# A decoder layer on one core: x1 and x2 of 13 groups turned in 32x32 blocks on VectorE and moved by 16 transfers each, with another order of a round's products

## The reference

```python
qkv = x @ w_qkv.T + b_qkv                      # 8 heads, no softmax
x = layernorm(x + ((q @ k.T) @ v) @ w_o.T + b_o)            # x1
q, k, v = x @ W_q.T + b_q, ctx @ W_k.T + b_k, ctx @ W_v.T + b_v   # 16 heads of 32
attn = softmax(where(mask == 0, -1e9, q @ k.T / sqrt(32)))
x = layernorm(x + (attn @ v) @ W_o.T + b_o)                 # x2
x_prev = x shifted by one row within a batch
xr, xk = mu * x + (1 - mu) * x_prev
out = sigmoid(xr @ W_r.T) * (square(relu(xk @ W_k.T)) @ W_v.T)
x = layernorm(x + out)                                      # y3
```

## Time and profile before

| | |
|---|---|
| median of 3 runs | 916.45 us (916.25 to 916.95) |
| profiled execution | 914.96 us, its span 912.9 us |
| granted TensorE clock | 0.998 of full |
| busy: TensorE, VectorE, ScalarE, GpSimd | 98%, 76%, 61%, 57% |

### The profile page before, as it was taken

One profiled execution on the slowest core, in us unless ns is written; L12 is line 12 of the kernel. 1 busy time (PEld: TensorE's weight loads), 2 busy tenths in 40 slices (PEclk: granted clock), 3 DMA queues, 4 the chain that ended last, 5 costly groups with the idle time before them and its releaser, 6 DMA issues.

```text
span 912.9 us, 23290 instructions
## 1 busy us (share of the span) xinstructions
PE 896.7 (98%) x8774; PEld 749.0 (82%) x8774; DVE 695.6 (76%) x1994; ACT 556.5 (61%) x1667; POOL 521.8 (57%) x505
## 2 busy tenths in 40 slices
PE   8999999999999999999999999999999999999997
PEld 7867766787788888888878888888888888888886
DVE  6688566578877878787877878787877777787775
ACT  7555236858675756575856666666665757575631
POOL 1045015759666666666675757566676767665420
PEclk9999999999999999999999999999999999999999
DMA  8792020113000001012101010101010100100001
GB/s 296 245 271 58 24 94 2 43 36 136 9 25 31 25 25 31 24 32 82 32 24 32 24 32 25 32 25 32 25 32 24 31 26 12 44 2 24 2 24 46
DMA packets 32332, 46.54 MB, mean 51 GB/s; under 512 B 3806, under 2 KB 16606, under 8 KB 32094
## 3 DMA queue, kind: packets, MB, share of 16 engines
q1 hardware_dynamic: 28622, 37.99, 12.8%
q10 hardware_dynamic: 3600, 7.08, 2.3%
HBM read 34.10 MB, written 9.70 MB: 48 GB/s over the span
## 4 chain that ended last, share of the span: by engine, by line
PE 75%; DVE 4%; POOL 4%; issue 4%; ACT 1%; POOLq 0%; ACTq 0%
PE dense L92 19%; PE dense L94 17%; PE dense L93 17%; PE turned L1664 5%; PE turned L1686 5%; PE scores L1650 4%; PE dense L1540 2%; PE turned L1668 1%; PE turned L1540 1%; POOL row_inv L1442 1%; POOL weight L1450 1%; PE scores L1546 1%; DVE mix_k_raw L1204 1%; PE dense L1557 0%; POOL prob_rest L1449 0%
## 5 line engine op out<-in xcount | busy, mean ns | idle before, releaser
L1442 POOL TENSOR_TENSOR row_inv<-row_sum,minus_one 128x4 f32<-128x4 f32 x128 | 152.6, 1192 | 190.1 <-ACT prob L818 190.0
L818 ACT ACTIVATE prob<-prob,row_min 128x154 f32<-128x154 f32 x512 | 209.6, 416 | 39.8 <-DVE row_min L1160 39.8
L1450 POOL TENSOR_TENSOR weight<-prob,row_inv 128x512 f32<-128x512 f32 x128 | 148.0, 1156 | 0.0
L1160 DVE CUSTOM_DVE_ANT_0 prob<-scores,mask_add 128x154 f32<-128x154 f32 x512 | 127.8, 312 | 4.0 <-PE scores L1650 3.7
L826 ACT ACTIVATE prob_t<-turned 128x512 f32<-128x512 f32 x128 | 76.0, 594 | 84.6 <-PE turned L1664 83.8
L818 ACT ACTIVATION_READ_ACCUMULATOR prob<-prob,row_min 128x1 f32 x512 | 98.3, 192 | 0.0
L1664 PE MATMUL turned<-ident,weight 128*128 128x128 f32 x512 | 76.9, 272 | 3.4 <-DVE o_t_lo L1167 3.0
L1664 PEld LDWEIGHTS turned<-ident,weight 128*128 128x128 f32 x512 | 61.2, 139 | 17.9 <-issue 6.3
L92 PE MATMUL dense<-mix_k_hi,ffn_wk_hi 128*128 128x256 f32 x256 | 75.3, 294 | 0.0
L92 PE MATMUL dense<-xt_hi,cross_wq_hi 128*128 128x256 f32 x256 | 75.2, 294 | 0.0
L94 PE MATMUL dense<-mix_k_hi,ffn_wk_lo 128*128 128x256 f32 x256 | 72.3, 283 | 0.0
(11 more groups left out here) (276 smaller groups left out, 2684.7 us busy)
## 6 DMA issues: line engine op xcount, KB each, us to landing
x_rows<-x_rows SPq DMA_DIRECT2D x32, 256.0 KB, 4.6
xt_raw<-x_cols SPq DMA_DIRECT2D x16, 512.0 KB, 3.8
out<-gate_then_y SPq DMA_DIRECT2D x15, 512.0 KB, 2.8
mask_in<-mask SPq DMA_DIRECT2D x16, 154.0 KB, 2.3
cross_wv<-cross_wv SPq DMA_DIRECT2D x2, 512.0 KB, 6.6
cross_wk<-cross_wk SPq DMA_DIRECT2D x1, 1024.0 KB, 9.3
self_wv<-self_wv ACTq DMA_DIRECT2D x1, 1024.0 KB, 7.3
self_wk<-self_wk ACTq DMA_DIRECT2D x1, 1024.0 KB, 9.6
```

What stands on the lines that cost most here:

```text
L818: m = act.activation(keys, keys, ACT.Exp, bias=row_min[:, buf, t, h:h + 1], scale=-1.0, accum_out=row_sum[:, buf, t, h:h + 1])
L1160: m = dve.tensor_tensor_reduce(exp_slot(n, u)[:, i * CTX:(i + 1) * CTX], s_bank[:, h, t * CTX:(t + 1) * CTX], mask_add[n % 2][:, t, :], -S ...
L1442: pool.tensor_tensor(row_inv[:, buf, t, :], row_sum[:, buf, t, :], minus_one[:], ALU.pow).then_inc(*p_inv.up)
L1450: pool.tensor_tensor(first, early, inv_early, ALU.mult).then_inc(*p_norm.up)
```

## The change

For 13 groups each (x1 of groups 3 to 15, x2 of groups 1 to 13) the transposes on TensorE go. VectorE turns each tile in 32x32 blocks (`turn`, one instruction of 128x512 for a tile), x1 into a buffer over `xt_hi`, x2 into one over the second half of o_t, and SP then moves the blocks to the partitions where they belong: 16 transfers for x1 (into `x_in`) and 16 for x2 (into x2t), each of 32 partitions x 1 KB. x1 is then split from SBUF with one `x1_high` (ScalarE, 128x1024) and one `x1_low` (VectorE, 128x1024), which replace two instructions each; `turned_x2` goes. The turned x stays in blocks of 32 columns: `q_product` reads its moving operand in eight runs of 32 columns, `take_q` puts the columns back in order, and `difference` becomes two instructions. It is now x_prev - x, with 1 - mu made once in the column constants. The raw difference lies in the buffer of mix k, so `blend(f, "r")` comes first.

Products come in another order, bank assignments and their waits change with them, and ScalarE's, VectorE's and GpSimd's orders follow. Two waits are new in `v_product`'s second half and in `q_product`: the first now waits for `r_gate(e, 1)`, the second for `x1_low(a)` and for the first `v_finish(e, 0)`. `exponentials`, `take_turned` and the rest are as before. On GpSimd `x_low` comes first, `scale(2, f)` moves ahead of the second `weigh`, and `scale(3, e)` to the end of the same round.

```diff
-    tile["x2t"] = mem.place("x2_t", [P, KT, 1 + GT])
+    tile["x2t"] = mem.place("x2_t", [P, 1 + GT // SQUARE, KT, SQUARE])
+    tile["x2_squares"] = mem.over("o_t_hi", "x2_squares", [P, 3, D], 4 * D)
+    tile["x1_squares"] = mem.over("xt_hi", "x1_squares", [P, TPG, D])
...
+        steady = {"y": (d1, d0), "o": (d1, d0), "k": (d0, d1), "r": (d0, d1), "q": (d0, d0), "v": (d0, d1)}
+        in_loop = lambda kind, n: kind in steady and first_of[kind] <= n <= past[kind]
+        bank = lambda kind, n, i: (steady[kind] if in_loop(kind, n) else last.get((kind, n), two[kind]))[i]
...
+            def move_x1(n):
+                sp.wait_ge(*tr1_mm.at(n))
+                for j in range(ROWS4):
+                    for i in range(ROWS4):
+                        sp.dma_start(x_in[j * SQUARE:(j + 1) * SQUARE, i, :],
+                                     x1_squares[i * SQUARE:(i + 1) * SQUARE, :, j * P:(j + 1) * P]).then_inc(*x1_back.up)
+
+            def move_x2(n):
+                sp.wait_ge(*tr2_mm.at(n))
+                sp.wait_ge(*carried.at(n))
+                for j in range(ROWS4):
+                    for i in range(ROWS4):
+                        sp.dma_start(x2_places[j * SQUARE:(j + 1) * SQUARE, 1 + i:2 + i + ROWS4:ROWS4, :],
+                                     x2_squares[i * SQUARE:(i + 1) * SQUARE, 0:3:2, j * P:(j + 1) * P]).then_inc(*x2_back.up)
...
                 if live(e - 1) and e - 1 < LAST:
                     store(e - 1)
+                if live(f) and moved_x2(f):
+                    move_x2(f)
...
+            def x1_high(n):
+                act.wait_ge(*x1_back.at(n - 3))
+                act.activation(xt_hi[:], x_in[:], ACT.Copy).then_inc(*x1t_hi_ok.up)
...
+                if g >= 2 and moved_x2(n - 1):
+                    act.wait_ge(*x2_back.at(n - 2))
...
-                x_high(a)
                 k_relu_half(e, 0)
                 take_turned(n, 0, 0)
-                k_high(e, 0)
                 exponentials(n, 1, 0)
+                x_high(a)
                 take_turned(n, 0, 1)
...
-                r_gate(e, 0)
+                exponentials(n, 2, 1)
+                k_relu_half(e, 1)
+                o_high(n, 1)
                 if n == 2:
                     weight_high("ffn_wv")
-                turned_x2(f, 0)
-                r_gate(e, 1)
-                x1t_high(a, 0)
-                o_high(n, 1)
-                x1t_high(a, 1)
-                turned_x2(f, 1)
+                k_high(e, 1)
                 exponentials(n, 3, 0)
-                k_relu_half(e, 1)
+                r_gate(e, 0)
                 take_turned(n, 2, 0)
+                x1_high(a)
                 exponentials(n, 3, 1)
-                k_high(e, 1)
-                mix_high(f, "k")
-                take_q(a, 0)
-                if a == GPB - 1:
-                    next_m_high(0)
                 take_turned(n, 2, 1)
                 take_rest(n, 2)
-                if a == GPB - 1:
-                    next_m_high(1)
+                r_gate(e, 1)
                 mix_high(f, "r")
                 if a == GPB - 1:
-                    next_m_high(2)
-                take_q(a, 1)
+                    for k in range(KT):
+                        next_m_high(k)
+                take_q(a, 0)
                 o_high(n, 2)
-                if a == GPB - 1:
-                    next_m_high(3)
...
+
+            def turn(to, rows, t):
+                return dve.transpose(to.rearrange("p (j k s) -> p k j s", j=ROWS4, k=KT),
+                                     rows[:, t, :].rearrange("p (k j s) -> p k j s", j=ROWS4, k=KT))
+
+            def turn_x1(n):
+                dve.wait_ge(*y_mm.at(n))
+                for t in range(TPG):
+                    dve.wait_ge(*ln_ok[1].at(n, t + 1))
+                    turn(x1_squares[:, t, :], x1[n % 2], t).then_inc(*tr1_mm.up)
+
+            def turn_x2(n):
...
+            for n in range(2, LAST):
+                a, f, e = n + 1, n - 1, n - 2
+                o_low(f, 3)
+                masked_min(n, 1, 0)
+                masked_min(n, 1, 1)
+                k_square(e, 0)
+                k_low(e, 0)
...
+                o_finish(f, 0)
+                o_finish(f, 1)
+                o_low(n, 0)
+                masked_min(n, 2, 0)
+                normalise(2, f, x2[f % 2])
+                turn_x2(f)
...
+                y_finish(a, 0)
+                masked_min(n, 2, 1)
+                y_finish(a, 1)
+                normalise(1, a, x1[a % 2])
+                turn_x1(a)
+                k_square(e, 1)
+                o_low(n, 1)
+                masked_min(n, 3, 0)
+                masked_min(n, 3, 1)
...
+                k_low(e, 1)
+                make_mask(a)
+                difference(f)
+                x1_low(a)
+                blend(f, "r")
+                v_finish(e, 0)
+                blend(f, "k")
+                carry(f + 1)
+                o_low(n, 2)
+                masked_min(a, 0, 0)
+                masked_min(a, 0, 1)
+                k_mix_low(f)
...
+                v_finish(e, 1)
+                normalise(3, e, y3)
...
+            def spread_product(to, weight, h, parts):
+                for i in parts:
+                    cols = slice((2 * h + i) * P, (2 * h + i + 1) * P)
+                    for k in range(KT):
+                        m = three_pass(pe, to[:, i * GT:(i + 1) * GT].rearrange("p (b s) -> p b s", s=SQUARE),
+                                       (weight[0][:, k, cols], weight[1][:, k, cols]),
+                                       (moving(xt_hi)[:, k], moving(xt_lo)[:, k]), first=(k == 0), last=(k == KT - 1))
...
-                        pe.wait_ge(*k_sq.at(n - 3, 2))
-                m = column_product(bank("q", n, h), w["cross_wq"], (xt_hi, xt_lo), h, parts)
+                    pe.wait_ge(*(x1_low_at(n) if moved_x1(n) else x1t_lo_ok.at(n)))
+                    if h == 0 and n >= 3:
...
-                    pe.wait_ge(*q_out.at(n + 3, t + 1))
+                    pe.wait_ge(*r_out.at(n, t + 1))
...
-                y_product(a, 0)
                 values(n, 0)
                 scores(n, 2)
+                y_product(a, 0)
+                transposes(n, 1, 0)
                 y_product(a, 1)
-                transposes(n, 1, 0)
-                r_product(e, 0)
                 transposes(n, 1, 1)
-                r_product(e, 1, early)
-                x2_turn(f, 0)
-                r_product(e, 1, late_half)
-                x1_turn(a, 0)
+                k_product(e, 1)
                 values(n, 1)
                 scores(n, 3)
-                x1_turn(a, 1)
-                x2_turn(f, 1)
-                k_product(e, 1)
+                r_product(e, 0)
                 transposes(n, 2, 0)
+                r_product(e, 1)
+                transposes(n, 2, 1)
+                v_product(e, 0)
+                v_product(e, 1, early)
                 q_product(a, 0)
-                transposes(n, 2, 1)
-                q_product(a, 1)
                 values(n, 2)
                 scores(a, 0)
-                v_product(e, 0)
+                v_product(e, 1, late_half)
                 transposes(n, 3, 0)
-                v_product(e, 1, early)
+                q_product(a, 1, (0,))
                 transposes(n, 3, 1)
-                v_product(e, 1, late_half)
+                q_product(a, 1, (1,))
                 values(n, 3)
                 scores(a, 1)
```

More of the change, by code:

```diff
@@ L30 @@
 PIECES = P // SIDE_ROWS
+SQUARE = 32
+ROWS4 = P // SQUARE
 EPS = 1e-5
@@ L1000, in act_program @@
                 take_rest(n, 3)
-                exponentials(a, 0, 0)
+                take_q(a, 1)
                 exponentials(a, 0, 1)
@@ L1144, in x1t_low, with x1_low @@
             def x1t_low(n, t):
-                cols = slice(t * P, (t + 1) * P)
                 dve.wait_ge(*x1t_hi_ok.at(n, t + 1))
-                dve.tensor_tensor(xt_lo[:, :, cols], by_k(bank("x1", n, t)), f32(xt_hi[:, :, cols]),
+                dve.tensor_tensor(spread(xt_lo)[:, t], squares(bank("x1", n, t)), f32(spread(xt_hi)[:, t]),
                                   ALU.subtract).then_inc(*x1t_lo_ok.up)
+            def turn(to, rows, t):
[7 more added lines that the diff above has]
+            def turn_x2(n):
+                dve.wait_ge(*o_mm.at(n))
+                for t in range(TPG):
+                    dve.wait_ge(*ln_ok[2].at(n, t + 1))
+                    turn(x2_squares[:, 2 * t, :], x2[n % 2], t).then_inc(*tr2_mm.up)
+            def x1_low(n):
+                dve.wait_ge(*x1_high_at(n))
+                dve.tensor_tensor(xt_lo[:], x_in[:], f32(xt_hi[:]), ALU.subtract).then_inc(*x1t_lo_ok.up)
             def masked_min(n, g, t):
@@ L1177, in carry @@
             def carry(n):
-                first, last = x2t[:, :, 0:1], x2t[:, :, GT:GT + 1]
+                first, last = x2t[:, 0, :, SQUARE - 1:SQUARE], x2t[:, GT // SQUARE, :, SQUARE - 1:SQUARE]
                 if n:
@@ L1265, in dve_program @@
             take_t(0)
```

(33 more changed lines are left out.)

154 lines of the change are left out of this document (76 added, 78 removed).

## The result

The changed kernel takes 1067.44 us, the median of 4 runs (1065.26 to 1069.2), against 916.35 (4 runs): a ratio of 1.1646, 95% interval 1.1619 to 1.1673. It is slower, as forecast, but by 151 us and not by 61, and it lies above the range that was given. Its profiled execution took 1069.2 us, with a span of 1067.3.

The account below looks back on a forecast made before the run. TensorE's queue bounds the 47.0 us round; without turns 45.8, plus 5.9 of waiting for x1's moved blocks, makes 51.7. 914.96 + 13 x 4.7 = 976, with 1.5 for the median 977.5 us; range 925 to 1050.

Parts of the forecast that it names:

- The round without the wait for x1: TensorE's loop round if everything else arrives in time: 45.8 us, 1.2 a round less than before.
- short waits: Two waits left on TensorE by the order: 0.3 us for scores(a, 0), 0.2 at the last weight transposes.
- The runs of 32 columns: q_product's moving operand read in runs of 32 columns on TensorE, taken at no cost.
- A turn: VectorE's turn of one 128x512 tile: 0.69 us, 2.8 a round for four.
- x2's squares: VectorE has x2's turned blocks ready to move 4.7 us after the first y_product starts.
- From x1_high to TensorE's start: ScalarE's steps from x1_high through the gate r_gate(e, 1): 4.0 us.
- The one long wait: TensorE waits about 6 us a round before v_product's second half, released by ScalarE's gate.
- One issue and its gap: Price of each of the 32 transfers a round on SP's queue: 0.50 us, within bounds of 0.42 and 0.9.
- The landing behind the last issue: Time from the end of SP's issues until x1_high can start: 2.0 us.
- The Trainium skill's 50 ns of dispatch: Under this rule the moves take 2.8 us and the rival of transfers in time, 900 us, holds: 12%.
- the clock at 1.00: TensorE's granted clock in the rounds stays at 1.00; if it falls with the idle time, the loss is larger.
- x2 was said to be in time: x2's moved blocks are back at 14.7 us in the round, ahead of VectorE's difference at about 15.9.

Follow-up runs that it names:

- four_each: Changed kernel with each move made by 4 transfers of 128 KB in place of 16 of 32 KB, values landing in wrong places: 913.21 us.
- by_dram_low_first: Changed kernel with moves through DRAM in 10 issues a round, x1_high behind r_gate(e, 1), x1_low between v_finish(e, 0)'s halves: 929.68 us.
- x2_alone: Kernel before, in its own order, with only x2 turned on VectorE and moved by 16 transfers, x1 left on TensorE: 924.65 us.
- two_queues: Changed kernel with x1's last 8 transfers issued by ScalarE just ahead of x1_high, the rest by SyncE: 1008.73 us.
- warm_all: Changed kernel with 96 unread matmuls of 128 columns put on TensorE before the wait of v_product(e, 1): 1055.47 us.
- by_dram_tuned: by_dram_low_first with x1_low in two halves, the first ahead of v_finish, and exponentials(a, 0, 0) put behind take_turned(n, 3, 0) on ScalarE: 911.12 us.

## Why the prediction was off

**Right.** The sign, the place and the chain. The round without the wait for x1 was put at 45.8, of which 45.2 were TensorE's work and 0.5 short waits (their sum is 45.7). Without any wait it is 46.0 (46.70 less 0.66 in four_each; 48.02 less 1.25 and 0.82 in by_dram_low_first), so the total was nearly right and the work 0.8 too low. Most of that lies in the products that the new order splits: in four_each's round at 559.78 the two tiles of v_product take 6.03 and not 5.76, and the second half of q_product, in two pieces, 3.34 and not 2.98. The runs of 32 columns cost nothing: the median 256-column matmul of cross_wq takes 283 ns, that of ffn_wk 281. A turn was put at 0.69; the median of 52 is 0.688. The Trainium skill's 311 ns ("VectorE: DVE Perf Modes", "The three transpose paths"), from which 1.24 had been estimated for a tile, is for another type and size, and scaling it by area would have been wrong by 0.55. x2's squares were ready at 5.2 and x1's at 12.45, put at 4.7 and 12.2. From x1_high to TensorE's start it was 4.06, put at 4.0. The one long wait is at v_product's second half, released by the gate, as named.

**The term that was mis-sized.** One issue and its gap were taken at 0.50. They take 0.66: 10.74 + 0.05 and 10.20 + 0.04 for 16 each, so 32 of them take 5.0 more than forecast. The single issue has a median of 0.597, and 16 of the 416 take over 1 us. The nearest row, a median of 0.58 for 64 partitions, was in hand, and it was talked down, since other issues in that stretch seemed stretched too; with it and the gap of 0.05 the same sum gives some 1032. The issues of 32 partitions took about as long as that row, at 32 KB and at 128 KB. The landing behind the last issue was 1.26 and not 2.0, since the 1.9 that the page of the profile gives counts from the issue's start; that took back the 0.5 by which x2's squares were later, and a little more. x1_high thus came at 27.47 and not at 22.7: 4.8 a round, 62 us in 13 rounds, is the larger part of the miss: 977.5 + 62 = 1040. The Trainium skill's 50 ns of dispatch ("DMA: Bandwidth & Descriptors", "Anatomy of one DMA"), which is given for the path through GpSimd, did not hold for SyncE's queue here, as the rows of before had said.

**The term that was left out.** The sum held the clock at 1.00, and only the last sentence of the prediction said that it might fall. In the round shown the lower clock cost 1.23 in the half of v_product (2.69 less 1.46) and 0.37 in the first four matmuls of q_product (0.85 less 0.48), 1.6, or 21 us in 13 rounds: 1061. Filling the wait gives 12 to 18 of these back. With 1040 alone the range would have held. The upper end came from the bounds of one price, and here a wait of ten us on TensorE had a second one. The rest, some 6 us, comes from rounds longer than the one worked out (58.84 on average against 58.19). The wait is 10.8 on average (140.7 / 13), not 10.55, which makes 3.5 us, and rounds of 60.1 and 59.8 (from 465.76 and 759.30) have a granted clock of 0.89, where the one shown has 0.91.

**Where nothing hides and where something did.** x2 was said to be in time at 14.7, difference at 15.9; it was not, VectorE waited 1.04 in difference(f) at 602.09. It cost nothing, since VectorE then waited 9.78 for x1_high. That x2 would pay by itself was wrong too, at least in the old order, as x2_alone shows: its expectation looked at x2's landing and named VectorE's added 1.3 us only as a rival. In the new order the forecast had followed VectorE's queue step by step, and its times held.

## What to carry to other kernels

Before a move is cut into many small transfers, multiply their number by the issue time of the nearest kind of transfer in the trace, and compare this with the time between the data being ready and its reader; bytes come second. A wait of several us on TensorE (3.4 to 10.6 here) is to be priced twice, once for itself and once for the matmuls behind it at the lower clock. And when the first cause is out of the way, read the queue of the next engine in the same place: here the same transfers in the same time gave 979, 930 and 911 us by three orders of VectorE and ScalarE (the last with x1_low in two halves).

## What the runs showed of the hardware

An issue on SyncE takes 0.60 from SBUF to SBUF with 32 partitions, at 32 KB as at 128 KB (medians of 0.597, and of 0.591 and 0.612), 0.34 to 0.37 for a store of 128 partitions to DRAM, and 0.43 (median) for a load of 32 partitions from it. Issues in ScalarE's queue take 0.62 (median of 104 in two_queues) and run beside its arithmetic.

TensorE's clock fell to the lower of its two levels, 1.2 GHz (512 columns in 0.43 us), with the idle times of 10.6, 4.0 and 3.4 us, and stayed at 2.4 GHz through the one of 1.25. The length of the wait alone does not decide it: in warm_all the granted clock is 0.97 in the rounds from 289.17 and 637.46, with waits of 1.5 and 1.3 us, and 1.00 in the one from 522.02, with a wait of 1.3.

VectorE and GpSimd hold each other up here. In by_dram_tuned, the second instruction of v_finish(e, 0) on VectorE stands beside GpSimd's low half of mix r:

```profile
628.68 2.87 DVE L1313 SCALAR_TENSOR_TENSOR gate_then_y<-gate_then_y,x 128x512 f32<-128x512 f32 x1
```

```profile
628.17 2.83 POOL L1553 TENSOR_TENSOR mix_r_lo<-mix_r_raw,mix_r_hi 128x1024 fp32r<-128x1024 f32 x1
```

Its shortest of 30 runs takes 0.69 (median 0.76), and here it ends 0.55 after GpSimd's does (631.55 and 631.00), as if it had only then begun. The Trainium skill, "SBUF — State Buffer", section "SBUF: two separate sides", says that a VectorE instruction with two inputs in SBUF and a GpSimd instruction that reads SBUF take turns at one pair of ports, each for its whole length; this trace agrees.
